# Reordering a few operations in the second chunks of a recommendation-tower kernel, and giving the third chunks' last tile a wait of its own

## The chip, the cores and the metric

The kernel runs on one core of a Trainium2 chip. The metric is the device time of one execution in microseconds (us); lower is better. Time before: 169.9 us, the median of 3 runs (169.72 to 170.08).

## What is computed

The reference, cut to what matters (512 examples, 26 tables of rows of 64 values, all in float32):

```python
x = layer_norm(dense_t @ Wd.T, gd, bd)                    # 512 x 128
e = stack([tbl_f[ids[:, f]] for f in range(26)], axis=1)  # gathered rows, 512 x 26 x 64
y = layer_norm(einsum('bnd,ed->bne', e, Ws), gs, bs)      # over the 128 values of a row
y = layer_norm(einsum('bne,pn->bep', y, Wsi), gsi, bsi)   # over 32 projections
T = concatenate([x[:, None, :], swapaxes(y, 1, 2)], axis=1)   # 33 vectors of 128
Z = einsum('bnd,bmd->bnm', T, T)[:, lower triangle]       # 528 products
z = layer_norm(Z @ Wl.T, gl, bl)[:, :384]
h = relu(concatenate([z, dense_t]) @ W_top1 + b_top1)     # layer 1, 512 wide
h = relu(h @ W_top2 + b_top2)                             # layer 2, 256 wide
out = h @ W_top3                                          # layer 3
```

## The kernel before, in words

The batch is cut into 4 granules of 128 examples, and each granule into 4 chunks of 32: 16 chunks, numbered n = 0 to 15, with c = n % 4 the place in the granule. "Second chunks" are those with c = 1 (n = 1, 5, 9, 13), "third chunks" those with c = 2. A chunk has 4 tiles of gathered rows when c = 0 and 3 otherwise; one tile takes two gathers.

GpSimd (POOL) gathers the rows, one indirect DMA after another (L332), into `G`. What happens to chunk n:

- TensorE (PE) transposes its tiles (`transpose_rows`, L1041) into `ps_gq`, ScalarE (ACT) copies them to `gt` (`gt_copy`, L424), and PE multiplies them by a Gram matrix (`gram_rows`, L1047).
- VectorE (DVE) turns this into a variance per row (`variance1`, L751 and L755), ACT takes the root (`deviation1`, L429), and DVE inverts it and scales the rows of `G` (`scale_rows`, L766 and L769).
- PE projects the scaled rows over the 26 fields (`project_fields`, L1059), ACT copies the result (`ut_copy`, L433), and PE maps it to 128 values in two halves (`embed`, L1072) in the two banks of `ps_y`.
- DVE moves the two halves to `V` with a bias added (`y_evacuate`, L783, one instruction for each half). ACT squares them (`square2`, L438), DVE sums (`variance2`, L790), ACT takes the root (`deviation2`, L442), and DVE inverts and scales `V` (`normalise2`, L797 and L799).
- PE forms the pair products (`pair_products`, L1079). ACT and DVE merge them into `zt` (`z_evacuate`, L448 to L450; `z_merge`, L841).

Once a granule, PE spreads the pairs (`spread_pairs`, L1167), ACT copies them (`z_copy`, L499), and PE projects them (`project_pairs`, L1121) and runs layers 1, 2 and 3 (L1137, L1147, L1155). ACT has `relu2` (L488) between layers 2 and 3, and `y_copy` (L493) after layer 3.

Each engine works through one list that is written out by hand. `slot(n)` is a stage of it: slot n starts chunk n's rows and carries forward the work of chunks n-1, n-2 and n-3. The loops run over slots 2 or 3 to 14; what stands before and after is written out. No engine passes an instruction that waits. Within slot 9, as an example of a second chunk, the lists are:

- PE: `transpose_rows(9)`, `project_fields(8)`, `gram_rows(9)`, `embed(8)`, `pair_products(7)`, `layer3(0)`. Slot 10 then begins with `transpose_rows(10)`, `project_fields(9)`, `gram_rows(10)`, `spread_pairs(1)`, `embed(9)`, `pair_products(8)`, `project_pairs(1)`.
- DVE: `z_merge(6)`, `normalise2(7)`, `variance1(9)`, `y_evacuate(8)`, `scale_rows(9)`, `variance2(8)`, `z_merge(7)`. Slot 10 begins with `x_slots(2)`, `normalise2(8)`.
- ACT: `z_evacuate(6)`, `gt_copy(9)`, `deviation2(7)`, `ut_copy(8)`, `deviation1(9)`, `relu2(0)`, `square2(8)`, `z_evacuate(7)`, `y_copy(0)`. Slot 10 begins with `gt_copy(10)`, `deviation2(8)`, `ut_copy(9)`, `z_copy(1)`.

`scale_rows(n)` keeps its reciprocals in bank 0 of `ps_y`, so it waits until the first half of chunk n-1 has been moved out. `normalise2(n)` with c = 0 keeps its own in bank 1, so `embed` of a second chunk waits for it (`pe.wait_ge(v_ready, n)`). SyncE (SP) starts the two parts of the weight load `wl` when the gathers of chunks 1 and 2 have landed.

## Time and profile before

| | |
|---|---|
| median of 3 runs | 169.9 us |
| the profiled execution | 170.86 us |
| its span (first to last recorded instruction) | 169.1 us |
| PE busy | 148.7 us, 88% of the span |
| DVE busy | 124.9 us, 74% |
| POOL busy | 100.5 us, 59% |
| ACT busy | 83.5 us, 49% |
| mean granted clock of PE, against full speed | 0.97 |

The profiled execution lasted 170.86 us, of which 1.76 us lie outside its span. Busy time overlaps between engines; it tells which engine is loaded, not which wait ends last. For that the chain of waits and the order in time are needed.

### The profile page before, as it was taken

How to read it: one execution, taken by the hardware profiler on the slowest of the kernel's cores; microseconds unless marked ns; L12 is line 12 of the kernel's file. 1: busy time of each engine (PE TensorE's matmuls, PEld its weight loads, DVE VectorE, ACT ScalarE, POOL GpSimd, SP SyncE). 2: the span in 40 equal slices, each digit the busy share in tenths (PEclk: the TensorE clock that was granted, in tenths of full speed). 3: DMA queues.
4: the chain of work that ended last, by engine and by line, in shares of the span. 5: the costliest groups of instructions: out<-in, count | busy, mean ns of one | idle time of the engine just before them, and what ended most of it. 6: DMA issues, size and time to landing. Idle time of an engine off the chain costs nothing.

```text
span 169.1 us, 3523 instructions
## 1 busy us (share of the span) xinstructions
PE 148.7 (88%) x1382; PEld 107.8 (64%) x1382; DVE 124.9 (74%) x256; ACT 83.5 (49%) x224; POOL 100.5 (59%) x109
## 2 busy tenths in 40 slices
PE   0398889987993999899999899999998999899995
PEld 0234557845562967556977565777866675589994
DVE  6494838987839678676599898485998987993153
ACT  3004243338676655876936555553537453652250
POOL 1777777777777777777777777777777400130000
PEclk9999999599999579999999999999999999999999
DMA  4913642615111111111111111111111100000000
GB/s 104 336 25 55 211 135 43 205 35 153 23 31 28 27 31 27 27 28 27 31 23 29 29 23 35 23 25 35 23 31 29 23 0 4 0 0 4 4 0 0
DMA packets 5728, 8.14 MB, mean 48 GB/s; under 512 B 2357, under 2 KB 3279, under 8 KB 5712
## 3 DMA queue, kind: packets, MB, share of 16 engines
q0 software_dynamic: 3328, 3.41, 11.1%
q1 hardware_dynamic: 1664, 3.65, 6.9%
q10 hardware_dynamic: 720, 0.85, 1.6%
q8 instruction: 11, 0.18, 0.5%
q14 instruction: 5, 0.04, 0.1%
HBM read 7.91 MB, written 0.00 MB: 47 GB/s over the span
## 4 chain that ended last, share of the span: by engine, by line
PE 49%; POOL 22%; DVE 11%; issue 9%; ACT 6%; DMA 2%; DVEq 0%
POOL G L332 22%; PE ps_tail L1121 8%; PE ps_y L1072 5%; PE ps_tail L1137 5%; PE ps_ut L1059 5%; PE ps_z L1079 5%; PE ps_gq L1047 4%; PE ps_z L1167 3%; DVE V L799 2%; PE ps_gq L1041 2%; PE ps_ut L1205 2%; DMA G<-in_table_dram,idx 2%; DVE var L755 1%; DVE var L790 1%; DVE V L783 1%
## 5 line engine op out<-in xcount | busy, mean ns | idle before, releaser
L332 POOL DMA_INDIRECT G<-in_table_dram,idx x104 | 98.4, 946 | 34.6 <-issue 31.4
L1059 PE MATMUL ps_ut<-S,G 128*128 128x192 f32 (+4 forms) x128 | 23.1, 329 | 0.4 <-DVE G L769 0.4
L1059 PEld LDWEIGHTS ps_ut<-S,G 128*128 128x128 f32 x128 | 21.4, 210 | 2.0 <-DVE G L769 1.5
L783 DVE TENSOR_TENSOR V<-ps_y,bias_y 128x512 f32<-128x512 f32 x32 | 20.5, 682 | 1.6 <-PE ps_y L1072 1.4
L790 DVE TENSOR_REDUCE var<-sq 128x32 f32<-128x1024 f32 x14 | 17.1, 1220 | 5.4 <-ACT sq L438 5.4
L1079 PEld LDWEIGHTS ps_z<-V 128*64 128x64 f32 x448 | 14.3, 136 | 10.3 <-DVE V L799 5.4
L438 ACT ACTIVATE sq<-V 128x1024 f32<-128x1024 f32 x14 | 14.9, 1061 | 10.9 <-DVE V L783 10.9
L1072 PE MATMUL ps_y<-ut,wcg 64*128 64x512 f32 x64 | 18.6, 655 | 1.4 <-ACT ut L433 0.7
L1047 PE MATMUL ps_gq<-gram,gt 128*128 128x128 f32 x104 | 16.2, 298 | 1.1 <-ACT gt L424 0.8
L1079 PE MATMUL ps_z<-V 128*64 128x67 f32 x448 | 16.2, 224 | 0.7 <-DVE V L799 0.5
L1047 PEld LDWEIGHTS ps_gq<-gram,gt 128*128 128x128 f32 x104 | 14.2, 208 | 1.9 <-issue 1.0
L429 ACT ACTIVATE sd<-var,eps 128x6 f32<-128x6 f32 (+1 forms) x16 | 4.8, 299 | 18.4 <-DVE var L755 18.4
L751 DVE TENSOR_TENSOR qg<-ps_gq,G 128x384 f32<-128x384 f32 (+1 forms) x16 | 9.4, 586 | 5.9 <-PE ps_gq L1047 5.9
L1041 PE MATMUL ps_gq<-eye,G 128*128 128x128 f32 x52 | 9.1, 289 | 4.3 <-DMA G<-in_table_dram,idx 4.3
L799 DVE TENSOR_TENSOR V<-V,ps_z 128x1024 f32<-128x1024 f32 x10 | 12.2, 1220 | 0.3
L1041 PEld LDWEIGHTS ps_gq<-eye,G 128*128 128x128 f32 x52 | 6.2, 145 | 9.3 <-DMA G<-in_table_dram,idx 6.2
L841 DVE COPY_PREDICATED zt<-mmask,ps_z 128x128 f32<-128x128 int32 x28 | 7.1, 313 | 6.5 <-ACT zt L450 6.5
L433 ACT COPY ut<-ps_ut 128x512 f32<-128x512 f32 x16 | 9.3, 583 | 4.9 <-PE ps_ut L1059 4.7
L1121 PE MATMUL ps_tail<-wl,zb 128*128 128x512 f32 x24 | 11.3, 608 | 0.3 <-issue 0.3
L424 ACT COPY gt<-ps_gq 128x384 f32<-128x384 f32 (+1 forms) x16 | 8.1, 506 | 6.8 <-PE ps_gq L1041 6.8
L338 POOL TENSOR_TENSOR V<-V,r_pool 128x1024 f32<-128x1024 f32 x1 | 1.9, 1916 | 14.1 <-DVE r_pool L805 14.1
L755 DVE TENSOR_REDUCE var<-qg 128x6 f32<-128x384 f32 (+1 forms) x16 | 9.4, 586 | 0.6
(179 smaller groups left out, 235.7 us busy)
## 6 DMA issues: line engine op xcount, KB each, us to landing
G<-in_table_dram,idx POOLq DMA_INDIRECT x104, 2.5
w1z<-in_w_z_dram SPq DMA_DIRECT2D x1, 768.0 KB, 4.2
wl<-in_wl_blocks_dram SPq DMA_DIRECT2D x1, 768.0 KB, 5.6
dns<-in_dense_t_dram ACTq DMA_DIRECT2D x1, 512.0 KB, 5.2
w1d<-in_w_d_dram SPq DMA_DIRECT2D x1, 512.0 KB, 5.5
wl<-in_wl_blocks_dram SPq DMA_DIRECT2D x1, 512.0 KB, 3.5
w2s<-in_w_dram SPq DMA_DIRECT2D x1, 512.0 KB, 3.5
wrow<-in_wsi_rows_dram SPq DMA_DIRECT2D x1, 208.0 KB
```

The source lines that it names most:

```text
L332: pool.indirect_dma_start(G[:, n // NC, j, g, :], None, table, bass.IndirectOffsetOnAxis(ap=idx[:, k:k + 1], axis=0)).then_inc(gathered[n ...
L438: act.activation(sq2[:, :, :].rearrange("p (b l) q -> p b l q", l=2), chunk_v(n), ACT.Square).then_inc(sq_ready, 1)
L755: dve.reduce_sum(var1[:, 0:2 * count], qg[:, 0:count * P].rearrange("p (t d) -> p t d", d=D), AX_X).then_inc(var1_ready, 1)
L783: dve.tensor_tensor(chunk_v(n)[:, g * CB // 2:(g + 1) * CB // 2, :, :], ps_y[:, g, :].rearrange("p (b l q) -> p b l q", l=2, q=NPROJ), bia ...
L790: dve.reduce_sum(var2[:, :], sq2[:, :, :], AX_X).then_inc(var2_ready, 1)
L799: dve.tensor_tensor(chunk_v(n), chunk_v(n), r2_at(n).rearrange("p (b l) -> p b l", l=2).unsqueeze(3).broadcast_to([P, CB, 2, NPROJ]), ALU. ...
L1041: mm = pe.transpose(ps_gq[:, i * P:(i + 1) * P], G[:, gp, j + i, :, :].rearrange("p g d -> p (g d)"), eye[:, :])
L1047: mm = pe.matmul(ps_gq[:, i * P:(i + 1) * P], gt[:, i * P:(i + 1) * P], gram[:, :], start=True, stop=True)
L1059: mm = pe.matmul(ps_ut[:, chunk % 2, col:col + width], G[:, gp, j, :, :].rearrange("p g d -> p (g d)"), S[:, j, :, :].rearrange("p s q -> ...
L1072: pe.matmul(ps_y[:, g, :], wcg[64 * g:64 * g + 64, :], ut[64 * g:64 * g + 64, :], start=True, stop=True).then_inc(y_ps, 1)
L1079: mm = pe.matmul(z_bank(n)[64 * ct:64 * ct + 64, w, s * SLOTS:(s + 1) * SLOTS], V[:, v, 3:SLOTS], V[:, v, :], start=True, stop=True)
L1121: mm = pe.matmul(ps_tail[:, :], zb[:, k, at] if k < PB else zx[:, at], wl[:, k, :], start=(k == 0), stop=(k == KB - 1))
```

## The change

Three edits. In second chunks from n = 9 on, ACT runs layer 2's activation (`relu2`) ahead of `deviation1`. In second chunks from n = 5 on, DVE runs `scale_rows(n)` between the two halves of `y_evacuate(n - 1)` instead of after both. In the third chunks, the two gathers of the last tile signal a semaphore of their own; PE transposes the first two tiles without waiting for them, and SP starts the second part of the `wl` load when the first two tiles have landed.

```diff
+        last_tile_gathered = [sem(f"last_tile_gathered{gp}") for gp in range(NG)]
...
-                sp.wait_ge(gathered[0][1 + h], 2 * len(batch(1 + h)) * 16)
+                sp.wait_ge(gathered[0][1 + h], 2 * (len(batch(1 + h)) - h) * 16)
...
-                            bass.IndirectOffsetOnAxis(ap=idx[:, k:k + 1], axis=0)).then_inc(gathered[n // NC][n % NC], 16)
+                            bass.IndirectOffsetOnAxis(ap=idx[:, k:k + 1], axis=0)).then_inc(
+                                last_tile_gathered[n // NC] if n % NC == 2 and j == js[-1] else gathered[n // NC][n % NC], 16)
...
-                deviation1(n)
                 if c == 1 and gp > 1:
                     relu2(gp - 2)
+                deviation1(n)
...
-            def y_evacuate(n):
-                for g in range(2):
+            def y_evacuate(n, halves=(0, 1)):
+                for g in halves:
...
-                y_evacuate(n - 1)
+                y_evacuate(n - 1, (0, 1) if c != 1 else (0,))
                 scale_rows(n)
+                if c == 1:
+                    y_evacuate(n - 1, (1,))
                 variance2(n - 1)
...
-                pe.wait_ge(gathered[gp][n % NC], 2 * count * 16)
+                split = n % NC == 2
+                pe.wait_ge(gathered[gp][n % NC], 2 * (count - split) * 16)
...
                 for i in range(count):
+                    if split and i == count - 1:
+                        pe.wait_ge(last_tile_gathered[gp], 2 * 16)
```

## Rows read from the trace of the kernel before

**Rows 1.** The page's first part: busy time, share of the span, instructions.
```profile
PE 148.7 (88%) x1382; PEld 107.8 (64%) x1382; DVE 124.9 (74%) x256; ACT 83.5 (49%) x224; POOL 100.5 (59%) x109
```

**Rows 2.** The chain that ended last, slots 9 and 10: start us, us, what.
```profile
94.97 0.52 ACT h L488 x2
...
96.61 1.31 PE ps_ut L1059 x8
97.94 0.94 PE ps_gq L1047 x6
98.87 1.34 PE ps_z L1167 x39
100.21 0.19 issue
```

**Rows 3.** The order in time, DVE, ACT and layer 3's PE row, slots 9 and 10.
```profile
94.55 1.28 DVE L783 TENSOR_TENSOR V<-ps_y,bias_y 128x512 f32<-128x512 f32 x2
94.67 0.30 ACT L429 ACTIVATE sd<-var,eps 128x6 f32<-128x6 f32 x1 [2.27 <-DVE var L755]
95.53 0.60 PE L1155 MATMUL ps_tail<-h,sm 128*1 128x128 f32 x4 [0.74 <-ACT h L488]
95.75 0.19 DVE L766 RECIPROCAL ps_y<-sd 128x6 f32<-128x6 f32 x1
95.86 1.06 ACT L438 ACTIVATE sq<-V 128x1024 f32<-128x1024 f32 x1 [0.38 <-DVE V L783]
95.97 0.55 DVE L769 TENSOR_TENSOR G<-G,ps_y 128x384 f32<-128x384 f32 x1
96.96 1.22 DVE L790 TENSOR_REDUCE var<-sq 128x32 f32<-128x1024 f32 x1 [0.44 <-ACT sq L438]
97.42 0.46 ACT L424 COPY gt<-ps_gq 128x384 f32<-128x384 f32 x1
98.10 0.51 DVE L841 COPY_PREDICATED zt<-mmask,ps_z 128x128 f32<-128x128 int32 x2
99.08 1.22 DVE L799 TENSOR_TENSOR V<-V,ps_y 128x1024 f32<-128x1024 f32 x1
```

**Rows 4.** The order in time, slot 13 (DVE) and slot 14 (PE).
```profile
126.38 1.28 DVE L783 TENSOR_TENSOR V<-ps_y,bias_y 128x512 f32<-128x512 f32 x2
...
132.23 1.13 PE L1072 MATMUL ps_y<-ut,wcg 64*128 64x512 f32 x4 [0.19 <-issue]
```

**Rows 5.** The order in time, slots 5 and 6 (DVE, PE).
```profile
66.21 1.22 DVE L799 TENSOR_TENSOR V<-V,ps_y 128x1024 f32<-128x1024 f32 x1
68.00 1.13 PE L1072 MATMUL ps_y<-ut,wcg 64*128 64x512 f32 x4
70.75 3.67 PE L1121 MATMUL ps_tail<-wl,zb 128*128 128x512 f32 x8 [0.34 <-issue]
```

**Rows 6.** The order in time: transposes of chunks 2, 5 and 14, chunk 14's last gather.
```profile
29.96 0.58 PE L1041 MATMUL ps_gq<-eye,G 128*128 128x128 f32 x3 [0.58 <-DMA G<-in_table_dram,idx]
...
55.23 0.90 PE L1041 MATMUL ps_gq<-eye,G 128*128 128x128 f32 x3 [2.65 <-DMA G<-in_table_dram,idx]
...
124.98 0.95 POOL L332 DMA_INDIRECT G<-in_table_dram,idx  x1 [0.30 <-issue]
...
127.89 0.55 PE L1041 MATMUL ps_gq<-eye,G 128*128 128x128 f32 x3
```

**Rows 7.** Gathers over the whole span: issue to landing.
```profile
DMA to landing us min/median/max: 2.4/2.5/4.9
```

**Rows 8.** Windows: A:B us, busy us (instructions) of PE, PEld, DVE, ACT, POOL; clock, DMA.
```profile
29.00:35.00 6.00, 5.29 (x25) 4.34 (x24) 5.75 (x18) 1.35 (x4) 4.58 (x5) 0.72 0.57 162
52.60:62.00 9.40, 6.77 (x37) 5.49 (x39) 6.71 (x13) 6.25 (x14) 7.27 (x8) 0.64 0.16 29
```

**Rows 9.** The order in time: field projections in slot 5 and in slot 9.
```profile
55.93 2.88 PE L1059 MATMUL ps_ut<-S,G 128*128 128x160 f32 x10
...
90.13 1.63 PE L1059 MATMUL ps_ut<-S,G 128*128 128x160 f32 x10 [0.21 <-DVE G L769]
```

## The prediction

> **What bounds the kernel now.** I read the page first. PE is busy 88% of the span and DVE 74% [rows 1], so PE is where a delay shows, but the share does not say which waits feed it. The chain of waits answers that. Up to 55.2 us it runs through the gathers: chunk 5's transposes stand idle for 2.65 us until its rows land [rows 6]. After that no transpose waits for a gather, and the chain runs through PE, with short excursions to ACT and DVE at the turn from second to third chunks. So anything before 55.2 us that costs less than 2.65 us costs nothing, and the change has to be judged in slots 9, 10, 13 and 14, with a look at slots 5 and 6.
>
> At slot 9 the reader should see two things. First, PE stops before layer 3: ACT's `deviation1` runs at 94.67, `relu2` only behind it (0.52 us from 94.97 [rows 2]), and layer 3 starts at 95.53 after 0.74 us of idle [rows 3]. The pair products before it have ended at 94.79, so 0.74 us are lost there. Second, and this decides the case, the order in time of DVE and ACT shows a second path beside the first: both halves of V are out at 95.83 (94.55 + 1.28), the square starts at 95.86, and behind it, with no gap, ACT runs the evacuation of the pairs, `y_copy` and the copy of chunk 10's transposes, 97.42 to 97.88 [rows 3]. PE's `gram_rows(10)` starts at 97.94, while the field projections ahead of it end at 97.92 [rows 2]. The two paths into it differ by 0.04 us. A gain on the one is worth nothing unless the other moves too.
>
> **The change, part by part.**
>
> *`relu2` ahead of `deviation1`.* It removes PE's 0.74 us wait: PE has left layer 2 before it projects chunk 8's fields at 90.13 [rows 9], and ACT is idle for the 2.27 us before 94.67 [rows 3]. Two activations take 0.52 us in the chain [rows 2], so they fit in there, layer 3 starts at 94.8, and the transposes of chunk 10 run from 95.3 to 95.85. The next step, `project_fields(9)`, needs scaled rows. These are ready at 96.52 (95.97 + 0.55) [rows 3] and it starts at 96.61 [rows 2]. By itself this edit therefore gives 0 to 0.1 us: the stall goes from layer 3 to the rows. I take 0. Nothing that ACT held up by the old order needed ACT then: it was idle for 0.38 us before the square [rows 3].
>
> *`scale_rows` between the halves.* The first half ends at 94.55 + 0.68 = 95.23 (1.28 us for two halves that overlap by 0.08 us, so 0.68 us each). Then come the reciprocal, 0.19 us, and the scaling, 0.55 us, each after a hand-over of 0.03 us like the one between 95.94 and 95.97 [rows 3]. Scaled rows are ready at 96.03 instead of 96.52, a gain of 0.49 us for `project_fields(9)`, which would run from 96.1 to 97.4. The second half, which overlaps the scaling by 0.08 us, runs from 95.95 to 96.63 instead of ending at 95.83. This is the price: 0.03 + 0.19 + 0.03 + 0.55 = 0.80 us on the second half of V.
>
> Who waits for the second half: ACT's square, and in ACT's list the pair evacuation, `y_copy` and `gt_copy(10)` are queued behind it. DVE's `variance2(8)`, `z_merge(7)` and `normalise2(8)` follow from the square. None of these has slack:
> - the square starts at 96.66, `gt_copy(10)` ends at 98.68 (the 2.02 us from 95.86 to 97.88 are back to back), and `gram_rows(10)` starts at 98.74 instead of 97.94: +0.80. PE idles from 97.4 to 98.74;
> - `variance2(8)` starts at 97.76 and `z_merge(7)` ends at 99.4, ahead of the spreading of pairs, now at 99.67;
> - `normalise2(8)` ends at 101.10 instead of 100.30 [rows 3], and `embed(9)` waits for it (a second chunk): 101.20 instead of 100.40 (100.21 + 0.19). The 0.19 us of idle before it [rows 2] is that same wait. Again +0.80.
>
> Both paths give the same 0.80 us, and what follows (pair projection, the square sum, `gt_copy(11)` and on to slot 12) starts from PE, so it all moves by 0.80 us.
>
> The Trainium skill (VectorE: DVE Perf Modes, "The DRAIN you can't avoid") says that a semaphore between two VectorE operations adds nothing to the flush that separates them anyway. The row shows 0.08 us of overlap between the two halves, which have no wait between them, and a gap of 0.03 us where there is a wait, so here the trace does not quite agree. By the rule a slot would cost 0.19 + 0.55 = 0.74 us.
>
> Slot 13 repeats slot 9, 31.83 us later: the halves at 126.38 against 94.55, `embed` at 132.23 against 100.40, with the same 0.19 us before it [rows 4]. Another +0.80 us.
>
> Slot 5 has the same reorder without the same effect. `normalise2(4)` ended at 67.43 (66.21 + 1.22) and would end at 68.2. `embed(5)` starts at 68.08 in the chain and would start near 68.3. That is +0.25 us, but the pair projection two steps on has an idle 0.34 us before it [rows 5], and it waits for ACT (the dense copy that follows `z_copy`, itself after the spreading, which is not moved). I take 0; without that cover it would be 0.25 us.
>
> *The third chunks' own wait.* It can help only where PE stands waiting for the last tile. Chunk 2 does, for 0.58 us [rows 6], but that lies ahead of the 2.65 us that absorbs it. Chunk 14's last gather is issued at 124.98; with the 2.65 us from issue to use that chunk 5 shows (52.58 to 55.23), it is in at 127.63, and the transposes start at 127.89 [rows 6]. With the delay from slot 9 they start still later, so there is nothing to split. Chunks 6 and 10 have more room. The extra wait inside the transposes isn't in this trace. From below it is 0; from above I take the 0.19 us of PE's longest gap marked "issue" between matmul groups in slot 10 [rows 2]. In slots 10 and 14 it lies ahead of PE's idle before the Gram product, and in slot 6 in the 0.34 us, so 0 either way.
>
> *SP.* The second part of `wl` (queued on SP behind the first, ahead of the last wait for layer 2's weights) starts two gathers, 2.5 us, earlier. It then shares the DMA engines with chunk 2's last two gathers. Landing takes 2.5 us as a rule and 4.9 us at worst [rows 7], so these could be up to 2.4 us late: under 2.65 us, absorbed. 0.
>
> Sum: 0 + 0.80 + 0.80 + 0 = +1.6 us (1.5 by the skill's rule). The profiled execution would go from 170.86 to 172.5 us (span 170.7), and the median, which lies 0.96 us below that execution, from 169.9 to **171.5 us**, +0.9%.
>
> **The rivals.**
>
> *Clock (0.15).* PE's idle 1.3 us in slot 10, right behind a short one for the rows, costs it the clock. For: the clock was at its low level (1.2 GHz) for about 3.4 us after a stretch of single-column matmuls and an idle of only 0.58 us (0.72 over 6 us is 2 x 0.28 x 6), and for 6.8 us after the 2.65 us idle (0.64 over 9.4 us) [rows 6, 8]. Against: these two stretches are 10.1 us at half the full clock, 5.1 us lost, and 3% of the span of 169.1 us is what the mean clock of 0.97 is short of 1, so nothing else in the trace, the 0.74 us idle at 94.8 included, made the clock fall. Price: ten projections took 2.88 us at the low level and 1.63 us at the high one [rows 9], so 3.4 us at the low level lose 3.4 x (1 - 1.63/2.88) = 1.5 us, and some 5.8 us of work lose 2.5 us. That gives 173.0 to 174.0 us for one fall, up to 174.5 for two short ones.
>
> *Half of it (0.12).* One of the two slots takes its delay, or part of it, in slack that I don't see, for instance where my hand-overs are off: 170.3 to 171.1, about 170.7 us.
>
> *Nothing (0.06).* DVE's second half is not what releases the square in time, or the delay is absorbed before the end: 169.6 to 170.2 us.
>
> *Faster (0.07).* The copy of chunk 10's transposes is not held behind the square, and PE uses both gains. The place is `gram_rows(10)` and `gram_rows(14)`: 0.49 us each. The second gain is limited by the gather: the last tile of chunk 14 lands at 127.63 against a start of 127.89, and here the split wait would matter, since two tiles go ahead; about 0.5 us is left in all, 169.4 us. It decides from the point where `gt_copy(10)` ends by 97.4, which asks for a square that starts at 95.4, before even the scaling has begun. ACT's idle 2.27 us with `relu2`'s input ready shows that its queue does not pass a waiting instruction. That speaks strongly against it.
>
> **How the numbers follow.** My forecast has a chance of 0.60. Its own range is 171.2 to 171.9 us (0.65 to 1.0 us for each slot, or the 0.25 us of slot 5 on top). For 8 in 10 I add the half case (0.12) and the lower end of the clock case: 170.5 to 173.0 us. A measurement of this kernel can tell about 0.2% (0.34 us) from no change. Faster by more than that: 0.08; within: 0.06; slower: 0.86.
>
> **What would show it.** In the changed trace: layer 3 (L1155) no longer waits for `relu2`; scaled rows (L769) of chunk 9 lie between two single L783 and come some 0.5 us earlier against the variance before them; the square's wait for V (0.38 us) grows to about 1.7 us; DVE's wait for the square in slot 9 grows from 0.44 to about 1.1 us; PE waits some 1.3 us for `gt_copy` in slots 10 and 14; `embed(9)` comes 0.8 us later and `embed(13)` 1.6 us. All of it fails if PE's Gram product in slot 10 starts right behind the projections; that would be the faster case. A granted clock under 1.00 between 95 and 140 us would be the clock case. Transposes of chunk 14 that wait for a gather would show that the kernel got ahead instead of falling behind.

## The result, and the profile after

The changed kernel takes 173.42 us (median of 5 runs, 172.50 to 173.78) against 170.08 us for the kernel before in the same comparison (5 runs, 169.72 to 170.20): ratio 1.0178, interval 1.0140 to 1.0216. It is slower by 3.3 us where 1.6 us were forecast. The single times of one and the same kernel spread (the kernel before: 121 runs, 169.4 to 172.3 us, median 169.9), so below the medians of all its runs count, and a stretch of a trace counts when several traces agree on it. The ratios and their intervals leave out executions more than 1.5% above the fastest of the same kernel (one of no_split, one of sp_full and two of sp_early_only among the changed kernels), so they are not the quotients of the medians.

The profiled execution of the changed kernel lasted 172.50 us, the shortest of its five, with a span of 170.7 us. These are the two figures forecast for a profiled execution, but that agreement misleads. The forecast counted from an execution of the kernel before that was 0.96 us above its median, and this one is 0.92 us below its own. That the two meet is luck.

The page's first part answers to [rows 1]:

```profile
PE 148.0 (87%) x1382; PEld 107.5 (63%) x1382; DVE 125.0 (73%) x256; ACT 83.6 (49%) x224; POOL 100.7 (59%) x109
```

PE works 0.7 us less and the span is 1.6 us longer. The loss is idle time of PE, not work.

The order in time, slots 9 and 10, answers to [rows 2, 3]. Source lines have moved: L785 is `y_evacuate`, L768 and L771 `scale_rows`, L440 `square2`, L426 `gt_copy`, L490 `relu2`, L1162 layer 3, L1048 `transpose_rows`, L1066 `project_fields`, L1054 `gram_rows`, L1079 `embed`, L1128 `project_pairs`, L792 `variance2`, L801 `normalise2`. In the other kernels the lines lie a few numbers apart.

```profile
92.11 0.63 ACT L490 ACTIVATE h<-ps_tail,sm 128x128 f32<-128x128 f32 x2
...
94.36 0.68 DVE L785 TENSOR_TENSOR V<-ps_y,bias_y 128x512 f32<-128x512 f32 x1
...
94.53 0.60 PE L1162 MATMUL ps_tail<-h,sm 128*1 128x128 f32 x4
...
95.14 0.20 DVE L768 RECIPROCAL ps_y<-sd 128x6 f32<-128x6 f32 x1
...
95.38 0.55 DVE L771 TENSOR_TENSOR G<-G,ps_y 128x384 f32<-128x384 f32 x1
95.85 0.68 DVE L785 TENSOR_TENSOR V<-ps_y,bias_y 128x512 f32<-128x512 f32 x1
...
95.98 1.33 PE L1066 MATMUL ps_ut<-S,G 128*128 128x192 f32 x8 [0.38 <-DVE G L771]
...
96.56 1.06 ACT L440 ACTIVATE sq<-V 128x1024 f32<-128x1024 f32 x1 [1.79 <-DVE V L785]
...
97.66 1.22 DVE L792 TENSOR_REDUCE var<-sq 128x32 f32<-128x1024 f32 x1 [1.13 <-ACT sq L440]
...
98.12 0.46 ACT L426 COPY gt<-ps_gq 128x384 f32<-128x384 f32 x1
...
98.63 0.94 PE L1054 MATMUL ps_gq<-gram,gt 128*128 128x128 f32 x6 [1.31 <-ACT gt L426]
...
99.78 1.22 DVE L801 TENSOR_TENSOR V<-V,ps_y 128x1024 f32<-128x1024 f32 x1
...
101.10 1.13 PE L1079 MATMUL ps_y<-ut,wcg 64*128 64x512 f32 x4 [0.19 <-issue]
```

Layer 3 has no wait any more. The waits went to the scaled rows (0.38 us) and to `gt_copy` (1.31 us), which stands behind the square, which waits 1.79 us for the second half of V. From the start of the first half to the end of the second DVE takes 2.17 us (95.85 + 0.68 - 94.36), where it took 1.28 [rows 3]. That is 0.89 us more, and from the first half to `embed` it is 0.89 us more too: 101.10 - 94.36 = 6.74 against 100.40 - 94.55 = 5.85.

Slot 13 and 14, answering to [rows 4]:

```profile
127.08 0.68 DVE L785 TENSOR_TENSOR V<-ps_y,bias_y 128x512 f32<-128x512 f32 x1
...
128.57 0.68 DVE L785 TENSOR_TENSOR V<-ps_y,bias_y 128x512 f32<-128x512 f32 x1
...
131.35 0.94 PE L1054 MATMUL ps_gq<-gram,gt 128*128 128x128 f32 x6 [1.31 <-ACT gt L426]
...
133.87 1.13 PE L1079 MATMUL ps_y<-ut,wcg 64*128 64x512 f32 x4 [0.24 <-issue]
```

The same again: 133.87 - 127.08 = 6.79 against 5.85, or 0.94 us more.

Slot 6, PE alone. [rows 5] show part of the same stretch:

```profile
63.74 0.49 PE L1048 MATMUL ps_gq<-eye,G 128*128 128x128 f32 x3
...
65.72 0.94 PE L1054 MATMUL ps_gq<-gram,gt 128*128 128x128 f32 x6 [0.42 <-ACT gt L426]
...
68.31 1.13 PE L1079 MATMUL ps_y<-ut,wcg 64*128 64x512 f32 x4 [0.32 <-issue]
...
70.56 3.67 PE L1128 MATMUL ps_tail<-wl,zb 128*128 128x512 f32 x8
...
74.92 0.49 PE L1048 MATMUL ps_gq<-eye,G 128*128 128x128 f32 x3
```

Here the Gram product of chunk 6 waits 0.42 us for `gt_copy`, and `embed(5)` a further 0.32 us. From chunk 6's transposes to chunk 7's it is 11.2 us. Kernels without the reorder in slot 5 take 10.5 to 10.6 us (below).

The early part, which answers to [rows 6, 7, 8]: SP's `wl` loads (the row's length runs from the issue of the first to the issue of the second), PE's transposes of chunk 2, the landing of the gathers issued between 26.4 and 30.3 us, and three windows.

```profile
22.58 5.41 SPq L306 DMA_DIRECT2D wl<-in_wl_blocks_dram  x2
```

```profile
29.50 0.67 PE L1048 MATMUL ps_gq<-eye,G 128*128 128x128 f32 x2
32.23 0.48 PE L1048 MATMUL ps_gq<-eye,G 128*128 128x128 f32 x1 [2.06 <-DMA G<-in_table_dram,idx]
```

```profile
DMA to landing us min/median/max: 2.4/2.9/4.5
```

```profile
29.00:35.00 6.00, 3.94 (x17) 3.54 (x17) 4.59 (x16) 0.88 (x3) 4.69 (x5) 0.50 0.44 149
50.00:66.00 16.00, 13.66 (x118) 10.15 (x118) 12.58 (x23) 11.26 (x30) 12.13 (x13) 0.89 0.15 29
94.00:140.00 46.00, 41.79 (x464) 30.45 (x458) 37.11 (x71) 23.27 (x67) 30.20 (x32) 1.00 0.13 25
```

From the issue of the first `wl` load to that of the second it is 5.41 us, where it was 7.73 us before, so the second starts some 2.3 us sooner. The gather issued beside it, at 27.72 us, is chunk 2's last, and it lands after 4.5 us. The kernel before has such a gather too, issued at 30.04 us beside the load's later start and landing after 4.3 us. But that one is chunk 3's, whose transposes start at 37.61 only. Two tiles are transposed at 29.50 without a wait, but the last stands at 32.23 behind 2.06 us of idle, where all three went at 29.96 [rows 6]. The granted clock over 29 to 35 us is 0.50, the low level of 1.2 GHz throughout (0.72 in [rows 8]). Behind 94 us it is 1.00.

### The profile page after: what moved, and what is told of

It reads as the page before. It is cut to its first block, busy times and chain, and to the rows that moved or that the text cites. A ratio compares the mean times of both kernels' runs of the same rounds, so it can differ in the third digit from the quotient of the medians.

```text
span 170.7 us, 3523 instructions
## 1 busy us (share of the span) xinstructions
PE 148.0 (87%) x1382; PEld 107.5 (63%) x1382; DVE 125.0 (73%) x256; ACT 83.6 (49%) x224; POOL 100.7 (59%) x109
## 3 DMA queue, kind: packets, MB, share of 16 engines
q0 software_dynamic: 3328, 3.41, 10.5%
## 4 chain that ended last, share of the span: by engine, by line
PE 47%; DVE 20%; ACT 11%; POOL 11%; issue 7%; DMA 3%; DVEq 0%
POOL G L333 11%; PE ps_tail L1128 8%; PE ps_z L1086 5%; PE ps_y L1079 5%; PE ps_tail L1144 5%; DVE V L801 4%; DVE V L785 4%; PE ps_gq L1054 4%; PE ps_z L1174 3%; ACT sq L440 3%; ACT gt L426 3%; PE ps_tail L1035 3%; DMA G<-in_table_dram,idx 3%; PE ps_ut L1066 2%; DVE var L757 2%
## 5 line engine op out<-in xcount | busy, mean ns | idle before, releaser
L1066 PE MATMUL ps_ut<-S,G 128*128 128x192 f32 (+4 forms) x128 | 23.2, 330 | 1.4 <-DVE G L771 1.4
L1066 PEld LDWEIGHTS ps_ut<-S,G 128*128 128x128 f32 x128 | 21.4, 210 | 3.1 <-DVE G L771 2.8
L792 DVE TENSOR_REDUCE var<-sq 128x32 f32<-128x1024 f32 x14 | 17.1, 1220 | 7.7 <-ACT sq L440 7.7
L440 ACT ACTIVATE sq<-V 128x1024 f32<-128x1024 f32 x14 | 14.9, 1062 | 14.1 <-DVE V L785 14.0
L785 DVE TENSOR_TENSOR V<-ps_y,bias_y 128x512 f32<-128x512 f32 x32 | 20.7, 682 | 0.7 <-PE ps_y L1079 0.5
L1086 PEld LDWEIGHTS ps_z<-V 128*64 128x64 f32 x448 | 14.3, 136 | 9.8 <-DVE V L801 6.2
L1079 PE MATMUL ps_y<-ut,wcg 64*128 64x512 f32 x64 | 18.1, 639 | 1.6 <-issue 0.8
L1054 PE MATMUL ps_gq<-gram,gt 128*128 128x128 f32 x104 | 15.6, 291 | 4.1 <-ACT gt L426 3.9
L1054 PEld LDWEIGHTS ps_gq<-gram,gt 128*128 128x128 f32 x104 | 13.7, 202 | 5.0 <-ACT gt L426 4.0
L1086 PE MATMUL ps_z<-V 128*64 128x67 f32 x448 | 16.2, 224 | 0.6 <-DVE V L801 0.5
L1048 PE MATMUL ps_gq<-eye,G 128*128 128x128 f32 x52 | 9.2, 288 | 5.0 <-DMA G<-in_table_dram,idx 5.0
L1048 PEld LDWEIGHTS ps_gq<-eye,G 128*128 128x128 f32 x52 | 6.4, 148 | 10.0 <-DMA G<-in_table_dram,idx 6.3
L426 ACT COPY gt<-ps_gq 128x384 f32<-128x384 f32 (+1 forms) x16 | 8.1, 508 | 8.9 <-PE ps_gq L1048 8.7
L801 DVE TENSOR_TENSOR V<-V,ps_z 128x1024 f32<-128x1024 f32 x10 | 12.2, 1220 | 0.3
L843 DVE COPY_PREDICATED zt<-mmask,ps_z 128x128 f32<-128x128 int32 x28 | 7.2, 313 | 5.9 <-ACT zt L452 5.9
L1128 PE MATMUL ps_tail<-wl,zb 128*128 128x512 f32 x24 | 11.3, 608 | 0.0
L340 POOL TENSOR_TENSOR V<-V,r_pool 128x1024 f32<-128x1024 f32 x1 | 1.9, 1918 | 15.5 <-DVE r_pool L807 15.5
```

The lines of the kernel that those rows point to most:

```text
L426: act.copy(gt[:, 0:width], ps_gq[:, 0:width]).then_inc(gt_sb, 1)
L440: act.activation(sq2[:, :, :].rearrange("p (b l) q -> p b l q", l=2), chunk_v(n), ACT.Square).then_inc(sq_ready, 1)
L785: dve.tensor_tensor(chunk_v(n)[:, g * CB // 2:(g + 1) * CB // 2, :, :], ps_y[:, g, :].rearrange("p (b l q) -> p b l q", l=2, q=NPROJ), bia ...
L792: dve.reduce_sum(var2[:, :], sq2[:, :, :], AX_X).then_inc(var2_ready, 1)
L801: dve.tensor_tensor(chunk_v(n), chunk_v(n), r2_at(n).rearrange("p (b l) -> p b l", l=2).unsqueeze(3).broadcast_to([P, CB, 2, NPROJ]), ALU. ...
L1048: mm = pe.transpose(ps_gq[:, i * P:(i + 1) * P], G[:, gp, j + i, :, :].rearrange("p g d -> p (g d)"), eye[:, :])
```

## The experiments

All times are medians in us, with the runs' range and number, and the ratio to the kernel before on the same chip with its 95% interval. The kernels come in five groups, and those of a group share the runs of the kernel before: 169.82 (23 runs) in the first, 170.28 (17), 169.84 (29), 169.81 (29) and 170.68 (11) in the others. The table has a row for each kernel's one trace: where PE starts the transposes of chunks 1, 3, 6 and 7 (T1 to T7, us), the tail (span less T7) and the mean granted clock over 50 to 66 us. "Reorder", "load" and "relu2" say which edits the kernel has; "load" is SP's earlier load.

| kernel | edits | T1 | T3 | T6 | T7 | tail | clock |
|---|---|---|---|---|---|---|---|
| the kernel before | | 22.6 | 37.6 | 64.5 | 75.1 | 94.0 | 0.79 |
| before_again | | 23.1 | 38.5 | 63.1 | 73.7 | 94.0 | 1.00 |
| before_warm | | 22.5 | 37.4 | 62.5 | 73.1 | 94.7 | 1.00 |
| relu_only | relu2 | 23.8 | 39.1 | 63.8 | 74.4 | 93.9 | 1.00 |
| merge_first | relu2 | 23.7 | 39.1 | 63.8 | 74.3 | 93.7 | 1.00 |
| split_only | load | 22.5 | 38.8 | 63.6 | 74.1 | 94.0 | 0.89 |
| sp_early_only | load | 22.4 | 39.3 | 64.1 | 74.7 | 94.0 | 0.89 |
| split_warm | load | 22.5 | 39.0 | 63.9 | 74.4 | 94.0 | 0.89 |
| no_reorder | load, relu2 | 22.6 | 39.3 | 64.1 | 74.7 | 93.9 | 0.89 |
| reorder_only | reorder | 22.5 | 37.4 | 62.5 | 73.8 | 95.8 | 1.00 |
| reorder_warm | reorder | 22.4 | 37.8 | 63.1 | 73.9 | 95.7 | 0.89 |
| sp_full | reorder, relu2 | 22.5 | 38.0 | 62.7 | 74.1 | 95.7 | 1.00 |
| no_split | reorder, relu2 | 24.4 | 39.8 | 64.4 | 75.9 | 95.9 | 1.00 |
| slot5_old | load, relu2, reorder but for slot 5 | 23.1 | 39.6 | 66.2 | 76.8 | 95.8 | 0.79 |
| changed kernel | all | 22.6 | 38.9 | 63.7 | 74.9 | 95.8 | 0.89 |
| after_again | all | 23.5 | 40.0 | 64.7 | 76.1 | 95.8 | 1.00 |
| gt_ahead | all | 22.4 | 40.2 | 64.9 | 76.2 | 95.8 | 1.00 |
| after_warm | all | 22.4 | 39.1 | 64.0 | 75.2 | 96.4 | 0.89 |
| after_fill | all | 22.5 | 38.9 | 63.8 | 75.0 | 95.7 | 0.89 |
| after_third | all | 22.6 | 38.8 | 63.7 | 74.8 | 95.8 | 0.89 |

### First group: the edits one by one

**relu_only**: the first edit alone.

```diff
-                deviation1(n)
                 if c == 1 and gp > 1:
                     relu2(gp - 2)
+                deviation1(n)
```

> The kernel before with ACT's edit alone: relu2 ahead of deviation1. Theory A and rival B alike: no more than 0.1 us of change (170.0 us), since layer 3 no longer waits 0.74 us but the field projections then wait for the scaled rows until 96.5. A rival, that the wait for layer 3 was on the path: -0.7 to -1.4 us.

Measured: 170.39 (169.65 to 172.12, 12 runs), 1.0028 [0.9993, 1.0063]. No change is measurable. The stall has moved, as forecast: the trace has no wait before layer 3 (93.99 us), and the field projections at 95.85 us wait 0.54 us for the scaled rows.

**reorder_only**: the second edit alone.

```diff
-                y_evacuate(n - 1)
+                y_evacuate(n - 1, (0, 1) if c != 1 else (0,))
                 scale_rows(n)
+                if c == 1:
+                    y_evacuate(n - 1, (1,))
```

> The kernel before with DVE's reorder alone: scale_rows between the halves of y_evacuate in second chunks. Theory A: the second half of V is 0.89 us later in slots 9 and 13 (the trace of the changed kernel shows 2.17 us from the first half's start to the second's end against 1.28 us), so +1.6 to +1.8 us, 171.7 to 171.9 us. Rival B: +3.3 us, near 173.4 us. relu2 stays behind deviation1, so PE still waits for layer 3's input, and its Gram product then follows the copy on ACT as before.

Measured: 171.33 (171.25 to 172.30, 6 runs), 1.0096 [1.0065, 1.0127]. The tail has grown by 1.8 us, the two slots of 0.9 us each. The median is 0.4 us below the range expected.

**no_split**: both edits above, without the third.

```diff
+                y_evacuate(n - 1, (0, 1) if c != 1 else (0,))
...
+                    y_evacuate(n - 1, (1,))
...
+                deviation1(n)
```

> The changed kernel without its third edit: relu2 ahead and the reorder, one semaphore for all gathers of a chunk, SP's load where it was. Theory A: +1.6 to +1.8 us over the kernel before, 171.7 to 171.9 us, the same as the reorder alone. Rival B: 173.4 us. A third theory, C (PE's longer idle in slots 10 and 14 costs it the clock in some executions): a spread of the single times of 1 us and more, and a granted clock below 1.00 between 95 and 140 us in the profile.

Measured: 173.27 (171.46 to 174.07, 6 runs), 1.0153 [1.0097, 1.0209]. The tail (95.9 us) is no longer than with the reorder alone. What this trace has more came before T1 (24.4 us), where neither edit does anything yet. The median is 1.4 us above theory A's range and beside rival B's value. But six runs from 171.5 to 174.1 us, at a clock of 1.00 behind 94 us in the trace, decide neither (see sp_full).

**split_only**: the third edit alone (the semaphore, both waits of PE, SP's earlier load).

```diff
+                sp.wait_ge(gathered[0][1 + h], 2 * (len(batch(1 + h)) - h) * 16)
...
+                pe.wait_ge(gathered[gp][n % NC], 2 * (count - split) * 16)
...
+                    if split and i == count - 1:
+                        pe.wait_ge(last_tile_gathered[gp], 2 * 16)
```

> The kernel before with the third edit alone: the last tile of third chunks on its own semaphore, PE's split wait, and SP's second wl load two gathers earlier. Theory A (the earlier load delays chunk 2's last tile by 2.3 us, 32.2 instead of 29.96, and this pushes PE's later work into a different pattern of granted clock, which is what the median of 173.42 us shows beyond the predicted 171.5): the median rises by 0.5 to 1.6 us over the kernel before, and the transposes of chunk 2's last tile start near 32.2. Rival B (the split is absorbed before 55.2 us, the reorder costs everything): within 0.34 us of the kernel before.

Measured: 170.30 (169.91 to 171.20, 12 runs), 1.0029 [1.0003, 1.0055]. Its transposes of chunk 2's last tile stand at 31.70 behind 2.11 us of idle. The same stretch as shown above for the changed kernel, PE:

```profile
63.61 0.49 PE L1046 MATMUL ps_gq<-eye,G 128*128 128x128 f32 x3
...
65.01 0.86 PE L1052 MATMUL ps_gq<-gram,gt 128*128 128x128 f32 x6
...
67.29 1.13 PE L1077 MATMUL ps_y<-ut,wcg 64*128 64x512 f32 x4
...
69.77 3.67 PE L1126 MATMUL ps_tail<-wl,zb 128*128 128x512 f32 x8 [0.26 <-issue]
...
74.14 0.49 PE L1046 MATMUL ps_gq<-eye,G 128*128 128x128 f32 x3
```

Without the reorder the Gram product follows the projections at once and `embed(5)` waits for nothing. The 0.26 us before the pair projection, the cover that the prediction counted on, is there, but T6 to T7 is 10.5 us and not 11.2.

### Second group: slot 5, SP's load, and two controls

**before_again** (the kernel before once more) and **after_again** (the changed kernel once more).

> The kernel before, unchanged, measured as if it were a change. It shows what a comparison of two equal programs gives. Theory D (the stretch up to 75 us differs from execution to execution with the moment at which PE's clock rises near 13 to 18 us): a median within 0.3 us of the kernel before, with single times from 169.5 to 172.3 us. If it comes out 0.5 us away, the 0.5 us of the runs with the split alone and with relu2 alone are no effect of theirs.

> The changed kernel, unchanged, beside its variants. All theories: +2.7 to +3.5 us over the kernel before. Theory A2: of these, 1.8 us lie behind 75 us (the reorder in slots 9 and 13), and 0.9 to 1.7 us ahead of it (the late last tile of chunk 2, and the reorder in slot 5, which costs 0.7 us when PE is behind the gathers).

Measured: 169.91 (169.56 to 172.07, 12 runs), 1.0001 [0.9961, 1.0042]; and 173.69 (172.42 to 174.34, 6 runs), 1.0194 [1.0132, 1.0256]. So T7 lies 1.4 us apart in two executions of the kernel before (75.1 and 73.7), and the tail doesn't move at all.

**slot5_old**: the changed kernel with slot 5 in the old order.

```diff
-                y_evacuate(n - 1, (0, 1) if c != 1 else (0,))
+                y_evacuate(n - 1, (0, 1) if c != 1 or gp < 2 else (0,))
                 scale_rows(n)
-                if c == 1:
+                if c == 1 and gp > 1:
                     y_evacuate(n - 1, (1,))
```

> The changed kernel, with slot 5 in the old order (the reorder in slots 9 and 13 alone). Theory A2: 0.5 to 0.8 us less than the changed kernel, because the distance from chunk 6's transposes to chunk 7's was 11.2 to 11.5 us in the traces with the reorder in slot 5 and 10.5 to 10.6 us in those without. Rival (slot 5 is covered, as predicted): no difference.

Measured: 173.73 (172.80 to 174.39, 6 runs), 1.0187 [1.0126, 1.0247]. PE and a window:

```profile
66.24 0.49 PE L1048 MATMUL ps_gq<-eye,G 128*128 128x128 f32 x3
...
76.76 0.49 PE L1048 MATMUL ps_gq<-eye,G 128*128 128x128 f32 x3
```

```profile
50.00:66.00 16.00, 14.04 (x110) 9.73 (x109) 12.49 (x22) 11.41 (x30) 12.27 (x13) 0.79 0.15 29
```

T6 to T7 is back at 10.5 us, so the 0.7 us are slot 5's. But the median has not fallen. The clock was low over part of 50 to 66 us, and three of the six runs have this kernel's lowest mean clock, 0.96 (174.20 to 174.39 us). The other three took 172.80, 172.92 and 173.26 us; the four runs of after_again that are above 0.96 took 172.42 to 173.77 us, median 173.5. That would be 0.6 us for slot 5, but from seven runs picked by their clock. The medians leave it open.

**sp_full**: the changed kernel with SP waiting for all of chunk 2's gathers, as before.

```diff
                 sp.wait_ge(gathered[0][1 + h], 2 * (len(batch(1 + h)) - h) * 16)
+                if h:
+                    sp.wait_ge(last_tile_gathered[0], 2 * 16)
```

> The changed kernel, but SP starts the second part of the wl load only when all of chunk 2's gathers have landed, as before; PE keeps its split wait. Theory A2: chunk 2's last tile is transposed near 30.0 again instead of 32.2 us, and the median falls by 0.4 to 1.0 us against the changed kernel. Rival B: no difference.

Measured: 172.11 (171.33 to 174.97, 6 runs), 1.0105 [1.0041, 1.0170]. The last tile of chunk 2 is transposed at 30.03 again. The median is 1.6 us below that of the changed kernel in the same group, though the ranges overlap. No_split, which has the load where it was as well, had 173.27 us, so 1.6 us is too much to read into six runs. The ten runs of these two that count for the ratios have a median of 172.1 us, 1.3 us below the 173.42 us of the changed kernel. SP's earlier load costs something that the prediction put at 0.

### Third group: which part of the third edit, and the two paths

**sp_early_only**: the kernel before with SP's earlier load; PE waits for the whole chunk ahead of its transposes.

```diff
+                sp.wait_ge(gathered[0][1 + h], 2 * (len(batch(1 + h)) - h) * 16)
...
+                pe.wait_ge(gathered[gp][n % NC], 2 * (count - split) * 16)
+                if split:
+                    pe.wait_ge(last_tile_gathered[gp], 2 * 16)
```

> The kernel before with the third edit's effect on SP alone: the last tile of third chunks has its own semaphore, PE waits for both before it transposes, and SP starts the second part of the wl load two gathers earlier. Theory A3 (SP's earlier load is what the third edit costs: it delays chunk 2's last tile by more than 2 us): the same as the split alone, +0.3 to +1.0 us over the kernel before, and chunk 2's transposes near 32 us. Rival: no change, and the split alone was 0.5 us slower by its wait inside the transposes.

Measured: 170.76 (169.71 to 172.94, 12 runs), 1.0052 [1.0034, 1.0071]. Chunk 2's transposes start at 31.80. The earlier load costs time without the split. Whether PE's split wait wins part of it back (170.30 in split_only) is not shown: the two intervals overlap. Where the idle time before chunk 5 should have taken up the delay, the order in time (PE, DVE, ACT) is this, first of before_warm (the kernel before with four products added near its start, fourth group), then of sp_early_only:

```profile
53.90 1.06 ACT L438 ACTIVATE sq<-V 128x1024 f32<-128x1024 f32 x1 [0.90 <-DVE V L783]
54.02 0.69 DVE L769 TENSOR_TENSOR G<-G,ps_y 128x512 f32<-128x512 f32 x1
...
54.94 0.55 PE L1045 MATMUL ps_gq<-eye,G 128*128 128x128 f32 x3 [2.37 <-DMA G<-in_table_dram,idx]
...
55.32 1.53 PE L1063 MATMUL ps_ut<-S,G 128*128 128x160 f32 x10
...
57.41 0.51 DVE L841 COPY_PREDICATED zt<-mmask,ps_z 128x128 f32<-128x128 int32 x2 [1.20 <-ACT zt L450]
...
60.40 1.28 DVE L783 TENSOR_TENSOR V<-ps_y,bias_y 128x512 f32<-128x512 f32 x2
```

```profile
55.04 0.55 PE L1046 MATMUL ps_gq<-eye,G 128*128 128x128 f32 x3 [0.91 <-DMA G<-in_table_dram,idx]
...
55.47 1.06 ACT L440 ACTIVATE sq<-V 128x1024 f32<-128x1024 f32 x1 [0.89 <-DVE V L785]
55.59 0.69 DVE L771 TENSOR_TENSOR G<-G,ps_y 128x512 f32<-128x512 f32 x1
...
56.33 2.54 PE L1064 MATMUL ps_ut<-S,G 128*128 128x160 f32 x10 [0.74 <-DVE G L771]
...
58.98 0.52 DVE L843 COPY_PREDICATED zt<-mmask,ps_z 128x128 f32<-128x128 int32 x2 [1.20 <-ACT zt L452]
...
61.97 1.28 DVE L785 TENSOR_TENSOR V<-ps_y,bias_y 128x512 f32<-128x512 f32 x2
```

Chunk 5's transposes start at 54.94 and 55.04: PE's idle time before them has given way, as forecast. But DVE and ACT are late, and stay late. ACT's square is at 55.47 against 53.90, DVE's scaled rows at 55.59 against 54.02, `z_merge` (L841, here L843), which waits 1.20 us for ACT in both, at 58.98 against 57.41, the halves of V at 61.97 against 60.40: 1.57 us each time. This chain does not pass through chunk 5's transposes, and PE, whose projections of chunk 4 had 0.61 us of slack to the scaled rows (54.02 + 0.69 = 54.71 against 55.32), now waits 0.74 us for them. The table says it for all kernels: T6 follows T3 by 24.7 to 25.2 us in 18 of 20 traces, whatever the gather of chunk 5 does, and by 26.6 to 26.9 us in the two with a clock of 0.79. Of the traces that start chunk 1 by 22.6 us, those without the early load have T3 at 37.4 to 38.0, those with it at 38.8 to 39.3 (and one at 40.2). From T1 to T3 it is 14.9 to 15.5 us in the nine traces without the early load and 16.2 to 17.7 in the eleven with it.

**no_reorder**: first and third edit.

```diff
+                deviation1(n)
...
+                sp.wait_ge(gathered[0][1 + h], 2 * (len(batch(1 + h)) - h) * 16)
...
+                        pe.wait_ge(last_tile_gathered[gp], 2 * 16)
```

> The changed kernel with DVE's order as before: relu2 ahead and the whole third edit. Theory A3: the stretch from chunk 7's transposes to the end of the span is 94.0 us as in the kernel before (95.8 us with the reorder), so the median lies 1.8 us or more below the changed kernel's 173.7 us: 170.3 to 171.9 us. Rival (the reorder costs little and the split most): 172.5 us or more.

Measured: 170.66 (169.90 to 171.09, 12 runs), 1.0046 [1.0028, 1.0063]. So the reorder makes the difference between 170.66 and the changed kernel's 173.4, 2.8 us, of which 1.8 us are the tail's.

**gt_ahead**: the changed kernel with `gt_copy` of chunks 10 and 14 ahead of the square, where ACT is idle.

```diff
                 deviation1(n)
+                if c == 1 and gp > 1:
+                    gt_copy(n + 1)
...
-                if not early:
+                if not early and not (c == 2 and gp > 1):
                     gt_copy(n)
```

> The changed kernel, with ACT's gt_copy of the third chunk (10 and 14) moved ahead of square2 into ACT's idle time. It frees the first of the two paths by which the late second half of V reaches PE (square, then gt_copy, then the Gram product). If both paths cost the same 0.8 to 0.9 us, as predicted, the Gram product starts right behind the projections, near 1.3 us earlier, but embed(9) still waits for normalise2(8): 0 to 0.2 us gained in all, 95.6 to 95.8 us from chunk 7's transposes to the end. Rival (the copy held behind the square is the whole price): back to 94.0 to 94.4 us there, 1.4 us or more gained.

Measured: 172.74 (172.02 to 174.24, 6 runs), 1.0178 [1.0143, 1.0213]. PE, slot 10:

```profile
98.45 0.86 PE L1056 MATMUL ps_gq<-gram,gt 128*128 128x128 f32 x6
100.65 1.41 PE L1176 MATMUL ps_z<-zt,eye 64*32 64x128 f32 x48 [1.34 <-DVE zt L845]
102.45 1.13 PE L1081 MATMUL ps_y<-ut,wcg 64*128 64x512 f32 x4 [0.38 <-issue]
```

The Gram product follows the projections with no wait. Its 1.34 us have gone to the spreading of pairs, which waits for DVE's `z_merge` (L845), itself behind `variance2` and the late square, and `embed(9)` comes no sooner. The tail is 95.8 us, as without the edit. Both paths cost the same 0.89 us, as the prediction had it.

**merge_first**: the kernel before with `relu2` ahead, `z_evacuate` ahead of the square and `z_merge` ahead of `variance2` in slots 9 and 13.

```diff
+                if c == 1 and gp > 1:
+                    z_evacuate(n - 2)
                 square2(n - 1)
...
+                if c == 1 and gp > 1:
+                    z_merge(n - 2)
                 variance2(n - 1)
```

> A try for a faster kernel: the kernel before with relu2 ahead of deviation1 and, in slots 9 and 13, ACT's z_evacuate of the chunk two back ahead of square2 and DVE's z_merge ahead of variance2, so that both lie in idle time in front of the square's end. It shortens both paths by 0.4 to 0.6 us; PE then ends the spreading of pairs at 100.2 and embed(9) follows without its 0.19 us: 0.2 us a slot, 0.3 to 0.5 us in all, 93.5 to 93.7 us from chunk 7's transposes to the end instead of 94.0 us. If the merge makes DVE late for variance2, no gain.

Measured: 169.78 (169.57 to 171.85, 12 runs), 1.0013 [0.9976, 1.0050]. The tail is 0.3 us shorter, but chunk 10's transposes, at 95.13 us, now stand 0.62 us for their gather: POOL is the next bound. No gain can be measured.

### Fourth group: is it the clock's start?

Four extra products of zeros near the start of PE's list, to see whether the early state of the clock makes the executions differ. The same edit on four kernels: before_warm, after_warm, split_warm (third edit), reorder_warm (second edit).

```diff
+                for _ in range(3):
+                    pe.matmul(ps_tail[:, 0:256], ones[:, :], dmat[:, 0:2, :], start=True, stop=True)
                 pe.wait_ge(wsis_ready, 1)
...
+                pe.matmul(ps_tail[:, 0:256], ones[:, :], dmat[:, 0:2, :], start=True, stop=True)
```

> The kernel before with four extra matmuls of zeros (128x256 columns) in PE's idle time at the start, 5 to 9.5 us; they change no result. Theory E (the single times spread from 169.5 to 172.3 us because PE's clock rises at different moments between 10 and 18 us): the clock rises earlier, nearly all times fall within 0.3 us of 169.6 us. Rival (the spread has another cause, the clock's falls near 30 and 54 us): the spread stays.

> The changed kernel with the same extra matmuls. Theory E: the spread shrinks, and the distance to before_warm is the steady 1.8 us and the third edit's 0.8 us: 2.6 us, 172.2 us. Rival (the edits interact ahead of 75 us): 3.3 us or more above before_warm.

> The kernel with the third edit alone and the extra matmuls. Theory E: 0.3 to 0.9 us above before_warm, with little spread, chunk 7's transposes at 74.1 to 74.7 us instead of 73.7. Rival: equal to before_warm, so that the third edit costs only in executions whose clock rises late.

> The kernel with the reorder alone and the extra matmuls. Theory E: 1.8 us above before_warm and nothing ahead of 75 us. Rival (slot 5's reorder costs too): 2.3 to 2.6 us above before_warm.

Measured: before_warm 169.93 (169.55 to 171.13, 12 runs), 0.9995 [0.9957, 1.0033]. after_warm 173.01 (172.25 to 174.74, 6 runs), 1.0148 [1.0081, 1.0215]. split_warm 170.62 (169.91 to 172.39, 12 runs), 1.0036 [0.9996, 1.0075]. reorder_warm 171.65 (171.35 to 172.52, 12 runs), 1.0086 [1.0051, 1.0120].

PE does reach its full rate sooner. The four recorded matmuls of 512 columns of the projection with `wd` take 1.88 us in all four traces (from 9.1 to 9.5 us), where they took 3.78 us (from 8.80 us) in the kernel before. Only the durations tell this: the granted clock reads 1.00 in both. All four traces start chunk 1 at 22.4 or 22.5 us, where six of the sixteen others start it at 23.1 to 24.4. In those six, four later matmuls of 512 columns, which start at 14.3 to 15.4 us, take 3.00 to 3.40 us instead of 1.88. But the medians stay within 0.5 us of those without the products (of 173.42 us for the changed kernel), and the runs still spread by 1.2 to 2.5 us. So the start is one source of the spread and not the one that decides. Two traces show something else. In before_warm, chunk 10's transposes wait for a gather:

```profile
95.00 0.55 PE L1045 MATMUL ps_gq<-eye,G 128*128 128x128 f32 x3 [0.86 <-DMA G<-in_table_dram,idx]
```

So the gathers set a floor. This execution is early at T7 (73.1), but cannot start slot 10 before 95.0 us; chunk 14's transposes, at 127.38 us, wait 0.99 us again. Against before_again, T7 to chunk 11's transposes takes 0.40 us more and from there to chunk 15's 0.29 us more, and the tail is 94.7 instead of 94.0 us. And in after_warm, PE in slot 14 and a window:

```profile
131.62 1.48 PE L1058 MATMUL ps_gq<-gram,gt 128*128 128x128 f32 x6 [1.31 <-ACT gt L426]
```

```profile
132.00:135.00 3.00, 3.00 (x56) 2.57 (x56) 2.93 (x8) 1.16 (x3) 1.03 (x2) 0.50 0.10 22
```

Right behind the 1.31 us of idle that the reorder makes, PE's clock is at its low level over 132 to 135 us. The Gram product takes 1.48 us instead of 0.94, and the tail is 96.4 instead of 95.8 us. This is the clock rival, at a price of 0.6 us, and in one trace of the seven that have this idle of 1.31 us in slots 10 and 14. The other six read 1.00 from 94 to 140 us.

### Fifth group: filling the idle time

**after_fill**: the changed kernel with two products between projections and Gram product in slots 10 and 14. They write over projections of the chunk that follows, so part of the values is replaced: the bank that the expectation calls free was not. **after_third** is the changed kernel as a control.

```diff
+                if c == 2 and gp > 1:
+                    for _ in range(2):
+                        pe.matmul(ps_ut[:, 0, 0:256], ones[:, :], dmat[:, 0:2, :], start=True, stop=True)
                 gram_rows(n)
```

> The changed kernel with two extra matmuls (128x256 columns, into the bank of ps_ut that is free then, their result not used) between the field projections and the Gram product of slots 10 and 14, about 0.9 us of the 1.31 us in which PE is idle there. Theory F (in part of the executions that idle costs the clock): the median falls by 0.3 to 1.0 us against the control. Rival (the whole of the rest lies ahead of 75 us): no difference beyond 0.2 us.

> The changed kernel once more, unchanged, as the control: 3.2 to 3.6 us over the kernel before, single times between 172.3 and 174.5 us. Of its profile, theory F expects in about one execution of three a granted clock below 1.00 between 95 and 140 us; the rival a late start of chunk 7's transposes (75 to 76.5 us) and a clock of 1.00 behind it.

Measured: 172.55 (172.15 to 173.66, 6 runs), 1.0133 [1.0082, 1.0184]; and 173.01 (172.37 to 173.67, 6 runs), 1.0158 [1.0107, 1.0208]. The difference is 0.46 us with ranges that overlap: inconclusive. No trace here has the late fall of the clock. The kernel before had 170.68 us in this group, 0.8 us above the median of all its runs, which is why after_third lies only 2.3 us above it.

## Why the prediction was right on the direction and wrong on the size

**The reorder in slots 9 and 13: right.** Forecast +0.80 us each, measured +0.89. In all traces with the reorder the tail is 95.7 us or longer, in all without it 93.7 to 94.7. The 0.09 us are mostly the hand-over behind the first half: 95.14 - 95.04 = 0.10 us, where I took 0.03 from the one between reciprocal and scaling. The sum is 0.10 + 0.20 + 0.04 + 0.55 = 0.89. The Trainium skill's rule (VectorE: DVE Perf Modes, "The DRAIN you can't avoid") that a semaphore costs nothing beyond the flush would have made it 0.74 us; the trace speaks against it more strongly than the one before did. The signs named for the trace all came: single L785 around the scaling, 1.79 us before the square, 1.13 us before `variance2`, 1.31 us before the Gram products. Only the scaled rows end 0.4 us earlier behind the variance (2.04 us against 2.44) instead of some 0.5.

**`relu2` ahead: right.** Layer 3's wait is gone and the tail of relu_only is 93.9 us. The wait for the scaled rows, 0.54 us in relu_only, took its place.

**Slot 5: the first step that failed.** "I take 0; without that cover it would be 0.25 us." T6 to T7 is 10.5 to 10.6 us in the ten traces without slot 5's reorder and 10.8 to 11.5 in the ten with it, mostly 11.1 and more: about +0.7 us. Behind T6, `embed(5)` starts after 68.31 - 63.74 = 4.57 us in the changed kernel and after 67.29 - 63.61 = 3.68 us in split_only. That is 0.89 us, the price of slots 9 and 13, and not 0.25. The cover before the pair projection did take up a part, but it was 0.26 us in split_only: (70.56 - 63.74) - (69.77 - 63.61) = 0.66 us are left. I had looked at `embed(5)` alone and not at `gt_copy(6)`, which stands behind the square there as `gt_copy(10)` does. And the slack was read from an execution whose clock was low (0.79 over 50 to 66 us), first the kernel before:

```profile
65.01 0.48 ACT L424 COPY gt<-ps_gq 128x384 f32<-128x384 f32 x1 [0.47 <-PE ps_gq L1041]
...
65.88 0.86 PE L1047 MATMUL ps_gq<-gram,gt 128*128 128x128 f32 x6
```

then split_only, at 0.89:

```profile
64.15 0.51 ACT L426 COPY gt<-ps_gq 128x384 f32<-128x384 f32 x1
```

In the first PE was late, so the copy waited 0.47 us for the transposes and still ended 0.39 us before the Gram product: 0.86 us of slack for a delay of 0.89. In the second the copy waits for nothing and ends 0.35 us before it (65.01 - 64.66). Slot5_old, the other trace at 0.79, has the wait too (1.38 us). Slot5_old brings the stretch back and not the median.

**SP's load: the second step that failed.** The mechanism was right: I wrote that chunk 2's last gathers could be up to 2.4 us late, and the last tile was 2.3 us late (32.23 against 29.96). "Under 2.65 us, absorbed. 0" was wrong. PE's idle time before chunk 5's transposes did shrink (1.44 us of it are left at 55.16), but the delay ran on through DVE and ACT, which had no slack there. T3 came 1.3 us later, and T6 with it. In the medians it is less: the 36 runs of the three kernels with the load and without the reorder (split_only, sp_early_only, split_warm) have 170.53 against 169.88 us, +0.65 us, which the gathers' floor near 95.0 us would explain, as it takes some of the delay from early executions. With the reorder it is the 1.3 us given under sp_full.

The clock has a share in it. Ahead of T3 the share is not small: gt_ahead's last tile of chunk 2 is no later than the changed kernel's (32.08 against 32.23 us), but its granted clock stays at 0.50 until 38 us, where the changed kernel has 0.93 over 35 to 38 us, and its T3 is 40.2 instead of 38.9. Sp_full, with the last tile in time (30.03) but 0.50 over 32 to 35 and 0.82 over 35 to 38 us, has T3 at 38.0, where reorder_only (0.76 and 1.00) has 37.4. So the load's own part of the 1.3 us may be nearer 0.9 (38.9 against 38.0). Why the low stretch lasts longer in some traces is open. Behind T3 the share is small: at 0.89 over 50 to 66 us T6 follows T3 by 24.8 to 25.2 us, at 1.00 by 24.7 to 25.1. Only 0.79 costs, 2 us, and it came once without the load and once with it.

**The third chunks' own wait: right.** It is harmless. In the changed kernel's traces it is used in chunk 2 alone; no_reorder uses it in chunk 14 as well, where the last tile waits 0.22 us at 127.27. That no transpose waits for a gather behind 55.2 us held for the profiled execution but not for others: chunk 14's wait 0.69 to 1.32 us in before_again, before_warm, relu_only and merge_first.

**The sum.** Traces alike at T1 can be added up. Starting chunk 1 by 22.6 us, before_warm has a span of 167.8 us, and the changed kernel and its control after_third have 170.7 and 170.6: +2.8 to 2.9. From before_warm to the changed kernel, T6 comes 1.2 us later (the load, with what the clock has in it), T6 to T7 is 0.6 us longer (slot 5), and the tail is 1.1 us longer: 1.8 for the two slots, less 0.7 that before_warm loses by waiting for gathers in slots 10 and 14. The profiled execution of the kernel before starts by 22.6 us as well, but with its clock of 0.79 it is 2.0 us late at T7 and has a span of 169.1 us. This is why the two profiled executions lie only the forecast 1.6 us apart. Gt_ahead, as early at T1, has 172.0 us by its late T3.

Executions that start late (T1 from 23.1 us) and have no low clock at 50 to 66 us lie further apart: 167.7 to 168.3 us in before_again, relu_only and merge_first, 171.8 and 171.9 in no_split and after_again, +3.5 to +4.2, though no_split has the latest start of all. This fits a floor that hides a late start from the kernel before and hides nothing of the others. The pooled medians (173.42 of 17 runs, 169.88 of 121) are 3.5 us apart, between the two. The same floor would explain why the reorder alone costs only 1.5 us in the median (171.42 of 18 runs against 169.88), less than the 1.8 us of its tail. That the floor is what makes the kernels react differently fits all these traces, but no run moved the floor itself; it was argued, not shown.

**The rivals.** The clock's came once, for 0.6 us instead of 1.5 and more. "Half", "nothing" and "faster" are excluded by the tails. **Open** stay the medians of slot5_old and no_split, how the 1.3 us before T3 divide between the late gather and the clock, and why some executions have the clock down over 50 to 66 us and others, of the same program, have not. None of the kernels is measurably faster than the kernel before.

## What to carry to other kernels

When an operation is put between the halves of another, follow who waits for the second half: here ACT's copy for the next Gram product and DVE's merge both did, and a gain for the reader of the first half was worth nothing. An idle time in front of one instruction absorbs only the delays that come through that engine. Here PE's 2.65 us gave way and the chain through DVE and ACT, with no slack beside it, carried the delay on. A cover read from one execution is no term of the sum: here slot 5's came from a trace in which the clock was low and PE late. And where a transfer sets a floor, a delay may cost early executions less than late ones.

## What the hardware showed that I had not expected

- A gather issued as a 768 KB load starts lands after 4.3 to 4.5 us instead of 2.4 (at 30.04 us in the kernel before, at 27.72 us in the changed one). A load that starts 2.3 us sooner thereby hit another chunk's gather, and made the transposes 2.3 us later.
- PE's clock was at its low level over 132 to 135 us, behind 1.31 us of idle, in one execution (after_warm), and not in the six others with the same idle.
- The hand-over between two DVE operations with a wait is 0.10 us behind the evacuation of one half (95.04 to 95.14 us), and 0.04 us between the reciprocal and the scaling (95.34 to 95.38).
